# Mid rows moved from SBUF to SBUF, input statistics taken from the bands, a new order on VectorE and a new lead

## The reference

```python
x = x + conv3x3(_gn(x), L0_conv_weight * mask)          # mask from sums of |weight| and a threshold
x = x + conv5x5(_gn(x), L1_conv_kernel) + L1_conv_bias  # written with an FFT in the reference

def _gn(v, G=16, eps=1e-05):       # mean and variance over 2 channels and the whole image
    g = v.reshape(B_, G, C_ // G, H_, W_)
    m = jnp.mean(g, axis=(2, 3, 4), keepdims=True)
    s = jnp.var(g, axis=(2, 3, 4), keepdims=True)
    return ((g - m) / jnp.sqrt(s + eps)).reshape(v.shape)
```

## Time and profile before

| what | value |
|---|---|
| median of 3 runs | 913.19 us (913.11 to 914.11) |
| the profiled execution | 912.25 us, its span 910.5 us |
| PE busy | 788.7 us, 87% of the span |
| DVE busy | 685.2 us, 75% |
| ACT / POOL busy | 324.1 us / 320.4 us |
| DMA | 183.74 MB, mean 202 GB/s |
| DMAs issued by SP for mid | 136 stores and 128 loads |

### The profile page before, as it was taken

The page is one execution under the profiler, slowest core; times in us unless marked ns, Lnnn a source line. Parts: engine busy times, 40 slices in busy tenths (PEclk is TensorE's granted clock), DMA queues, the critical chain, the costliest instruction groups (busy, mean ns, idle before and its releaser), DMA issues.

```text
span 910.5 us, 108496 instructions
## 1 busy us (share of the span) xinstructions
PE 788.7 (87%) x52262; PEld 697.5 (77%) x52262; DVE 685.2 (75%) x1050; ACT 324.1 (36%) x417; POOL 320.4 (35%) x146
## 2 busy tenths in 40 slices
PE   1544578999999999999999999999999999998874
PEld 1433366888888889898888888898888888987774
DVE  5784534988889897979798888979797979673410
ACT  0212023344443343444434444334344443443231
POOL 0300004443434344444444243434444444434332
PEclk9877678999999999999999999999999999999998
DMA  8948943898989999998989898989989687856423
GB/s 185 224 114 213 247 115 87 226 243 221 247 202 261 209 244 238 220 252 215 246 221 243 209 247 207 265 202 244 245 217 250 166 204 182 211 149 165 100 61 77
DMA packets 72927, 183.74 MB, mean 202 GB/s; under 512 B 13248, under 2 KB 13504, under 8 KB 64704
## 3 DMA queue, kind: packets, MB, share of 16 engines
q1 hardware_dynamic: 68576, 179.45, 80.6%
q10 hardware_dynamic: 4320, 3.96, 2.1%
HBM read 116.23 MB, written 67.14 MB: 201 GB/s over the span
## 4 chain that ended last, share of the span: by engine, by line
PE 51%; DVE 31%; issue 8%; DMA 3%; SPq 3%; DVEq 1%; ACTq 1%; ACT 1%; POOL 0%; POOLq 0%
PE psum L687 51%; DVE x L549 5%; DVE bn_out L563 4%; DVE mid L571 4%; DVE bn_in L475 4%; DVE mid_bands L534 3%; DMA x_own<-x_dram 2%; DVE gscale L526 2%; DVE x_lo L557 2%; DVE deviation L511 1%; DVEq L573 1%; DVE product L509 1%; SPq L207 1%; ACTq L374 1%; DVE product L513 1%
## 5 line engine op out<-in xcount | busy, mean ns | idle before, releaser
L300 POOL TENSOR_TENSOR mid<-mid,conv_out 128x512 f32<-128x512 f32 x128 | 310.1, 2455 | 553.3 <-ACT conv_out L333 540.1
L687 PE MATMUL psum<-x_hi,s 32*32 32x512 f16 x25600 | 377.1, 381 | 19.7 <-ACTq L374 9.5
L687 PEld LDWEIGHTS psum<-x_hi,s 32*32 32x32 f16 x25600 | 338.6, 88 | 50.6 <-issue 15.5
L687 PE MATMUL psum<-x,s 32*32 32x512 f16 x13824 | 232.1, 396 | 47.1 <-DVE x L549 15.9
L687 PEld LDWEIGHTS psum<-x,s 32*32 32x32 f16 x13824 | 177.7, 88 | 99.8 <-issue 57.4
L687 PE MATMUL psum<-x_lo,s_hi 32*32 32x512 f16 x12800 | 186.5, 380 | 7.1 <-issue 7.1
L687 PEld LDWEIGHTS psum<-x_lo,s_hi 32*32 32x32 f16 x12800 | 175.5, 88 | 12.9 <-issue 8.3
L557 DVE TENSOR_TENSOR x_lo<-mid_bands,x_hi 128x2560 f16<-128x2560 f32 x32 | 104.0, 3251 | 49.9 <-PE psum L687 44.5
L549 DVE TENSOR_TENSOR x<-x_bands,x 128x2304 f16<-128x2304 f32 x32 | 102.8, 3213 | 38.8 <-PE psum L687 38.8
L571 DVE SCALAR_TENSOR_TENSOR mid<-psum,unscale,x_own 128x512 f32<-128x512 f32 x128 | 87.0, 742 | 46.5 <-PE psum L687 46.1
L333 ACT ACTIVATE conv_out<-psum,bias,unscale 128x512 f32<-128x512 f32 x128 | 94.2, 769 | 52.9 <-PE psum L687 52.9
(11 more groups left out here) (74 smaller groups left out, 162.8 us busy)
## 6 DMA issues: line engine op xcount, KB each, us to landing
x_own<-x_dram SPq DMA_DIRECT2D x128, 256.0 KB, 6.8
out_dram<-mid SPq DMA_DIRECT2D x128, 256.0 KB, 4.1
mid_bands<-mid_scratch SPq DMA_DIRECT2D x96, 320.0 KB, 7.5
mid_scratch<-mid SPq DMA_DIRECT2D x120, 256.0 KB
x_bands<-x_dram SPq DMA_DIRECT2D x96, 288.0 KB, 5.5
mid_bands<-mid_scratch SPq DMA_DIRECT2D x32, 288.0 KB, 5.3
x_bands<-x_dram SPq DMA_DIRECT2D x32, 272.0 KB, 6.3
every_mv<-mv_scratch ACTq DMA_DIRECT2D x15, 256.0 KB
```

The lines of the kernel that those rows point to most:

```text
L300: nc.gpsimd.tensor_tensor(m, m, conv_out[:, b, :], ALU.add).then_inc(out_added, 1)
L687: ins = nc.tensor.matmul(psum[quad(j), bank + i, :].rearrange("p (a w) -> p a w", a=A), w[quad(i), at, :], src[quad(i), A * j + dy:A * (j ...
```

## The change

- Mid no longer goes through DRAM. SP copies each block of four rows from `mid` to its place in `mid_bands` (`move_mid`, 16 DMAs of 32 partitions by 2 KB), and the halo rows when an image is complete (`move_edges`, 14 DMAs of 32 by 1 KB). `mid_bands` holds three halves.
- `stats_in` reads `x_bands`, which now holds six halves and is loaded far ahead; `x_own` holds two.
- `take_conv3` uses two instructions of 1024 columns.
- DVE's order in the steps is new, and ACT takes the first root of an even step ahead of `high3`.
- The lead is written anew: image 2's statistics go by DRAM like those of later images, and PE's mixes and `keep_warm` stand between the second and third conv3 visit of each lead step.

```diff
-X_SLOTS, MID_SLOTS = 6, 5
+X_SLOTS, MID_SLOTS = 2, 5
+XB_SLOTS, MB_SLOTS = 6, 3
+PIECES = 2
...
+            def move_mid(h):
+                sp.wait_ge(mid_made, PIECES * (h + 1))
+                for i in range(Q):
+                    for j in range(Q):
+                        move_rows(h, i, j, h, i, slice(0, A), 2 + A * j)
...
-            load_own(0)
-            load_own(1)
-            sp.dma_start(mix[:, :], mix_dram).then_inc(mix_loaded, 16)
-            load_bands(x_bands, 0, x, 1, x_bands_in)
+            load_bands(0)
+            load_bands(1)
+            sp.dma_start(mix[:, :], mix_dram).then_inc(mix_loaded, 16)
+            load_bands(2)
+            load_bands(3)
+            load_own(0)
...
-                if has3(s + 2):
+                if has3(s + XB_SLOTS):
                     sp.wait_ge(norm1, s + 2)
-                    load_bands(x_bands, s + 2, x, 1, x_bands_in)
+                    load_bands(s + XB_SLOTS)
                 if has3(s):
+                    move_mid(s)
+                    if s % 2:
+                        move_edges(s // 2)
+                    if has3(s + X_SLOTS):
                         load_own(s + X_SLOTS)
...
+                if gathered:
+                    take_root(gathered[0])
+                if s == 2:
+                    take_root(("mid", 0))
+                if has3(s + 1):
+                    high3(s + 1)
...
                 if has3(s + 1):
                     normalize3(s + 1)
+                if has5(s + 1) and s % 2:
+                    normalize5(s + 1 - LAG)
...
+                if gathered and s > LAG:
+                    dve.wait_ge(mv_in, 16 * exchange_number(s - 1))
+                    group_stats(gathered[0])
+                    scale_of(gathered[0])
+                if has3(s):
+                    take_conv3(s)
+                if has5(s + 1) and not s % 2:
                     normalize5(s + 1 - LAG)
                 if has3(s):
                     stats_out(s)
+                if exchanged(s):
+                    aggregate("mid", s // 2, None if len(exchanged(s)) > 1 else mv_ready)
+                    if len(exchanged(s)) > 1:
+                        aggregate("x", (s + 3) // 2, mv_ready)
+                if len(gathered) > 1:
+                    group_stats(gathered[1])
+                if has3(s + 5):
+                    stats_in(s + 5, range(BANKS))
+                if len(gathered) > 1:
+                    scale_of(gathered[1])
...
+            with nc.body("lead_low2", valid_engines=only):
+                mix_mean(("mid", 0))
+                mix_variance(("mid", 0))
+                keep_warm(6)
+                pe.br("lead_inner3")
```

More of the change, by code:

```diff
@@ L394, in _ @@
                     weights5(s5_hi)
-                if gathered:
-                    take_root(gathered[0])
                 if has5(s + 1):
@@ L568, in take_conv3 @@
                     dve.wait_ge(out_stored[h % MID_SLOTS], 16 * Q * (h // MID_SLOTS))
+                dve.wait_ge(x_own_in[h % X_SLOTS], 16 * Q * (h // X_SLOTS + 1))
                 dve.wait_ge(c3_whole, 2 * h + 2)
[L570 to L572 removed]
+                each = BANKS // PIECES
+                for p in range(PIECES):
+                    at = slice(each * p, each * (p + 1))
+                    nc.vector.scalar_tensor_tensor(mid[:, h % MID_SLOTS, at, :],
+                                                   psum[:, X3_BANK + at.start:X3_BANK + at.stop, :], unscale[:, 0:1],
+                                                   x_own[:, h % X_SLOTS, at, :], ALU.mult, ALU.add).then_inc(mid_made, 1)
                 dve.drain().then_inc(bank3_go, 1)
@@ L576, in stats_out @@
                 for b in range(BANKS):
-                    stats_mid(h, b)
+                    dve.wait_ge(mid_made, PIECES * h + b * PIECES // BANKS + 1)
+                    nc.vector.bn_stats(bn_out[:, h % 2, b, :], mid[:, h % MID_SLOTS, b, :]).then_inc(bn_mid, 1)
             def normalize3(h):
@@ L647, in _ @@
                     low3(s)
+                if s == LAG:
+                    dve.wait_ge(mv_in, 16)
+                    group_stats(("x", 2))
+                    scale_of(("x", 2))
                 if has3(s + 1):
                     normalize3(s + 1)
-                if has5(s + 1) and not gathered:
+                if has5(s + 1) and s % 2:
+                    normalize5(s + 1 - LAG)
+                if s == LAG:
+                    stats_in(6, range(BANKS))
+                if gathered and s > LAG:
+                    dve.wait_ge(mv_in, 16 * exchange_number(s - 1))
+                    group_stats(gathered[0])
+                    scale_of(gathered[0])
@@ L651, in _ @@
+                if has3(s):
+                    take_conv3(s)
+                if has5(s + 1) and not s % 2:
                     normalize5(s + 1 - LAG)
                 if has3(s):
-                    take_conv3(s)
                     stats_out(s)
-                if gathered:
-                    dve.wait_ge(mv_in, 16 * ((s - 1) // 2))
-                    group_stats(gathered[0])
-                    if has3(s + 4):
-                        stats_in(s + 4, range(0, 2))
-                    scale_of(gathered[0])
-                    normalize5(s + 1 - LAG)
-                    if len(gathered) > 1:
-                        group_stats(gathered[1])
-                    if has3(s + 4):
-                        stats_in(s + 4, range(2, BANKS))
-                    if len(gathered) > 1:
-                        scale_of(gathered[1])
-                elif has3(s):
-                    if has3(s + 4):
-                        aggregate("mid", s // 2)
-                        stats_in(s + 4, range(BANKS))
-                        aggregate("x", (s + 3) // 2, mv_ready)
-                    else:
-                        aggregate("mid", s // 2, mv_ready)
+                if s == LAG:
+                    stats_in(7, range(BANKS))
@@ L780, in _ @@
             pe.wait_ge(mix_loaded, 16)
-            mix_group(("x", 0))
-            keep_warm(8)
-            pe.wait_ge(w_bound, 2)
-            over_partitions(X5_BANK + 1, bound[:, 1:2])
+            mix_mean(("x", 0))
+            mix_variance(("x", 0))
+            keep_warm(11)
             pe.wait_ge(w3b_go, 1)
@@ L800, in _ @@
                 last3()
-                pe.br_lt(visit, 3, on_true="lead_inner3", on_false="lead_mix")
-            with nc.body("lead_mix", valid_engines=only):
+                pe.br_lt(visit, 3, on_true="lead_low", on_false="lead_next")
+            with nc.body("lead_low", valid_engines=only):
+                pe.br_eq(step, 0, on_true="lead_low0", on_false="lead_low12")
+            with nc.body("lead_low12", valid_engines=only):
+                pe.br_eq(step, 1, on_true="lead_low1", on_false="lead_low2")
+            with nc.body("lead_low2", valid_engines=only):
[3 more added lines that the diff above has]
+                pe.br("lead_inner3")
+            with nc.body("lead_low1", valid_engines=only):
+                pe.wait_ge(w_bound, 2)
+                over_partitions(X5_BANK + 1, bound[:, 1:2])
+                keep_warm(6)
+                pe.br("lead_inner3")
+            with nc.body("lead_low0", valid_engines=only):
+                mix_mean(("x", 1))
+                keep_warm(6)
+                pe.br("lead_inner3")
+            with nc.body("lead_next", valid_engines=only):
                 pe.nop().then_inc(bank3_go, -1)
```

207 lines of the change are left out of this document (98 added, 109 removed).

## The result

The changed kernel takes 881.05 us (median of 4 runs, 877.01 to 885.18), the kernel before beside it 913.35 (913.11 to 914.11): a ratio of 0.9645, 95% interval 0.9598 to 0.9693. The forecast was 874.6, the range 862 to 892. Sign and range were right; 6.5 us of the forecast gain did not come.

What follows compares the result with a forecast made beforehand. It took PE's gaps as the bound: DVE overloaded and mid's DRAM way in the lead, DVE late in odd steps. 18 + 19.4 + 1.2 = 38.6 off 912.25 gives 873.6, plus 0.94: 874.6 us, range 862 to 892.

Steps and rivals of the forecast that it cites:

- the lead wins half: Rival: edges land late or ACT's wait in step 3 is uncovered; 8 to 10 us instead of 18, 883 to 885; chance 0.14.
- Lead and step 3: Steps 0 to 3: 16.8 us from an earlier step 3, less 0.3, plus 1.5, gives 18 us (8 to 23).
- Start: First statistics need 0.23 MB more, 1.0 to 1.3 us later; PE's first step at about 27.2 instead of 26.18.
- Step 0: Lead: DVE has less between low3 and take_conv3, so step 1 can start at about 42 instead of 44.86.
- The price of a move: SP's issue of one move from SBUF to SBUF: 0.45 us taken, 0.47 to 0.82 by the nearest rows.
- Step 3: the cover: ACT's new wait of some 4.5 us falls on PE's 4.78 us on issue: costed at 0.3, 4.5 if uncovered.
- The steady pair: Steady steps: both PE waits of the odd step go; 1.54 us for each of 12 pairs, 19.4 us with steps 28 and 29.
- The 0.4 us for late statistics: Steady even step: loss allowed for gathered statistics landing after DVE asks, taken between 0 and 1.0 us.
- SP in a pair: Steady part: 46 moves take 21 us and 24 other DMAs 17, 38 of 47.4 us, so moves stay off the path.
- moves cost SP too much: Rival: at 0.82 us a move a pair takes 54.7, about 977; chance 0.07, shared with any other new slower bound.
- Tail: Step 32: earlier root wins 0.8 us of PE's pause, the visit behind it may get time back; 1.2 us (0 to 2.4).
- The signs named: Profile after: main loop near 73 us, step 4 near 126, moves 0.4 to 0.5 us, pair 47.5 to 48, DMA near 147 MB.

Runs made afterwards that it cites:

- f2_stats_in_gap: Changed kernel without keep_warm in the lead, nine matmuls ahead of conv5 in steps 32 to 34, half 5 loaded early, its and half 4's statistics in step 2: 865.76 us.
- e3_lead_fixed: Changed kernel with the even half's edge moves first, half 5 loaded before the moves, statistics of halves 4 and 5 in step 0: 885.1 us.
- f3_all: As f2_stats_in_gap, with the halo rows of the even half moved first: 866.71 us, ratio 0.9502 to the kernel before.
- e4_order_alone: Kernel before, mid still through DRAM and the old lead, with only the new order of the steady steps on DVE and ACT: 906.74 us, ratio 0.9933.

## Why the prediction was right or wrong, point by point

- **The number and the mechanism.** 881.05 lies inside the range, and 0.05 us outside the stretch from 868 to 881 to which the forecast gave 0.45. What happened is the rival "the lead wins half", which had a chance of 0.14: the edges landed late, and ACT's wait in step 3 was not covered. Lead and step 3 gained 11.1 us instead of 18 and the tail lost 2.2 instead of winning 1.2; the steady part, 1.6 us better than forecast, made up for some of it. That the time still came so near the forecast is in part luck.
- **Start.** Forecast 27.2, measured 27.30. Right.
- **Step 0: the cost of a new block of code.** Step 1 was to start at 42 and started at 46.35. The step that failed is "these end close to the end of `low3`, so they cost 0 to 0.8 us": PE came to `lead_low0` 5.12 us late, on "issue". The forecast had named this only as a possible loss of up to 4.8 us and left it out of its sum: the Trainium skill (Runtime: NRT & Kernel Launch, section "Instruction fetch mechanics") has taken branches out of the loaded code stall. The trace agrees that there is a stall at such a branch, 5.12 us long. A branch alone does not make it: `e6_no_warm` takes 18 matmuls out of the three blocks (the profile counts each fp32 one twice, 36) and leaves every branch, and the wait is gone. With the matmuls it shows in step 0 only, not at the first branch to the blocks of steps 1 and 2. `lead_low0` stands behind the blocks of the other two in the code. That it lay too far ahead with the matmuls in them fits this, and was not tested by itself.
- **The price of a move.** 0.45 was assumed, 0.63 to 0.69 measured, inside the bounds of 0.47 to 0.82; the 0.45 lay below those bounds, with no reason given. I took the number of pieces as what sets a price and wrote that the DMAs of 32 pieces that write SBUF all cost 0.43 to 0.47. They do not, even in the kernel before. SP's timeline there, for a DMA of 32 pieces from DRAM in the steady part (0.77 us each):

```profile
283.35 3.08 SPq L213 DMA_DIRECT2D x_bands<-x_dram  x4
```

  All these rows had DRAM at one side, too. The 23 moves ahead of `normalize5` took 15.5 us (23 x 0.676) instead of 10.35. With 3.9 us of later start (59.94 instead of 56) and 1.6 instead of 3 us for landing this gives 5.2 + 3.9 - 1.4 = 7.7 of the 8.1 us by which step 3 was late (81.57 instead of 73.5; the forecast's own chain ended at 74).
- **Step 3: the cover.** ACT's wait was costed at 0.3, because PE had stood 4.78 us on "issue" at that point, and it was said to cost 4.5 if that cover is gone. The wait was 6.19 us: the 4.5 of the forecast and the 1.71 for which DVE stood for half 5 at 88.07, which loads behind the 30 moves. And the cover was none: without the wait (`f2_stats_in_gap` at 75.93, and likewise in `e3_lead_fixed` and `f3_all`) all 288 matmuls run in one piece, with no "issue" in them. PE stands for DVE right ahead of them; in the kernel before it stood for DVE too, but still in the lead's code (at 89.67). That the code is fetched in this wait fits all of these, and was not tested by itself. The whole step came out close all the same (51.8 against 52.9 by the sum), and that was luck: "issue" elsewhere fell from 14.3 to 13.0 us, nearly as forecast, but with ACT's wait all waits of the step add up to 19.2 us, as before (19.1), where the forecast had 17.9. The 2.4 us won are time of the matmuls themselves, which was in no term of the sum: the last 217 of conv5's low image took 3.6 us behind waits of 1.6 and 1.7, and had taken 6.1 behind waits of 2.6 and 4.4. What ACT's wait costs shows beside `f2_stats_in_gap`, where step 3 lasts 46.8 us: 5 us, not 0.3.
- **The steady pair.** Forecast 47.5 to 48 us, measured 47.73 (572.71 / 12). DVE's chain holds to within 0.8 us: `take_conv3` starts at T + 14.2 (338.48, forecast 13.4), and the next `low5` at T + 26.4 (350.68), as forecast. The pair's parts, in the odd step from 300.66 and the even one from 324.30:

```profile
307.15 3.64 DVE L572 TENSOR_TENSOR x<-x_bands,x 128x2304 f16<-128x2304 f32 x1
310.85 2.25 PE L711 MATMUL psum<-x,s 32*32 32x512 f16 x144
324.30 4.60 PE L711 MATMUL psum<-x,s 32*32 32x512 f16 x288
334.66 1.08 DVE L530 SCALAR_TENSOR_TENSOR product<-every_mv,mix 128x128 f32<-128x128 f32 x1
347.34 0.20 ACT L334 ACTIVATE root<-gvar 128x1 f32<-128x1 f32 x1 [1.77 <-DVE gvar L538]
```

  `low3` ends 10.1 us after the odd step's start (forecast 10.2), and PE takes it without a wait. `group_stats` starts at T + 10.4 and the second root at T + 23.0 (forecast 10.3 and 22.5). PE waits for `low3` twice between 134 and 760 us, 2.5 us in all; in the other profiles with these steady steps none to four times, up to 4.9 us, so it is just in time, no more. The 0.4 us for late statistics were not needed.
- **SP in a pair.** 38 of 47.4 us was the forecast; it is nearly all. 46 moves take 29.2 us (19.01 in one step and 10.19 in the other), and the rows of SP stand nearly back to back. That was named as a sign that the forecast is wrong, and it wasn't, but only just:

```profile
298.57 10.19 SPq L225 DMA_DIRECT2D mid_bands<-mid  x16
```

  The other 24 DMAs take 17.8 us here, so SP needs 47.0 of the 47.7 us. The forecast put the limit at c = 0.70, against the old pair of 49.36; against the 47.73 that came it is (47.73 - 17.8) / 46 = 0.65, and a move cost 0.635. The rival "moves cost SP too much" missed by less than 3% in the price.
- **Tail.** The pause of 3.69 us shrank to 2.94 as forecast, but behind it the 400 matmuls took 7.38 us still, and the two that had taken 5.7 before took 7.37 and 6.99: 21.7 against 18.8 us for the three, which with the 0.75 won is the loss of 2.2. What failed is the assumption that the short pause gives the fast visit back. Over the eight profiled kernels with the changed layout and these pauses of 2.9 to 3.7 us, 18 of 24 such visits took 6.98 us or more, the others 5.7 or 5.8; with nine matmuls in the pause (four kernels) all 12 took 5.7 or 5.8. With the old layout 2 of 6 were slow (kernel before and `e4_order_alone`), one of them behind 2.93 us. So a visit can be as slow behind 2.9 us as behind 3.69, and the -2.2 us of the table are partly the draw of two executions: two fast visits of three before, none after.
- **The signs named.** Besides the starts and the price above, DMA was to be near 147 MB and moved 150.5. DVE waits for `every_mv` in no even step of the steady part, and the first pass through the loop stalls less than before (13.0 against 19.1 us).

## What to carry to other kernels

Two edits can each be worth little and much together: look which wait comes last once the first is gone, and what would then be late (here DVE's order, and behind it the statistics, late on a crowded DMA). Put work that only waits for data into the gaps in which an engine stands anyway, at a place where its data has landed; an in-order engine makes everything behind it wait. Don't count an old stall as cover for a new one until you know what caused the old one.

## What the runs showed of the hardware

- Issuing a DMA of 32 pieces costs SP 0.48 us from DRAM to SBUF in the lead (3.83 / 8) and 0.495 for halo rows, but 0.77 for `x_bands` in the steady part (3.08 / 4 before, 3.06 / 4 after), so the number of pieces does not set the price by itself; from SBUF to SBUF it costs 0.63 to 0.69, at 1 KB and 2 KB a piece alike.
- PE's first pass through code costs up to 6.8 us at a time on "issue" (in `e3_lead_fixed`, ahead of 126.19), and nothing in the 288 matmuls at the start of step 3 where PE had stood for DVE right ahead of them (`e3_lead_fixed`, `f2_stats_in_gap`, `f3_all`).
- After a pause of 2.9 us PE may or may not run its next 400 matmuls slower (5.7 to 5.8, or 7.0 to 8.7 us). In step 3, behind 9.72 us without work, the granted clock is 0.50 (the level of 1.2 GHz), and 144 matmuls take 4.07 us (81.57); in the steady part, at 1.00 (2.4 GHz), they take 2.25 (310.85). The window from 82 to 85 us:

```profile
82.00:85.00 3.00, 3.00 (x139) 2.31 (x112) 3.00 (x6) 0.00 (x0) 0.00 (x0) 0.50 0.97 233
```

  With 2.27 us of matmuls in that pause it was always 5.7 to 5.8.
- The gathered statistics needed up to 8.9 us from issue to landing with DMA at 224 GB/s (`e4_order_alone`), and at most 5.0 to 5.8 in each even step of the steady part at 187 GB/s (the changed kernel).
